# A four-part graph network on one core: dense layers interleaved, stream-back sums copied by ACT and added by GpSimd, third norm in four pieces

## The reference, cut to what matters

```python
# x: (6250, 128); 100000 edges (src, dst), dst sorted; edge_attr (E, 16), type (E,), weight (E,)
x = layernorm(x + segment_sum((x @ W)[src] * (edge_attr @ edge_w), dst) + b)
x = layernorm(x + relu(segment_sum(einsum('ni,rio->nro', x, W1)[src, type] * weight, dst) + bias))
ew = sigmoid(gelu(concat(x[src], x[dst]) @ mlp_w1 + mlp_b1) @ mlp_w2 + mlp_b2)   # self loops get 1
dinv = rsqrt(segment_sum(ew, dst))
x = layernorm(x + segment_sum((x @ conv_w)[src] * dinv[src] * ew * dinv[dst], dst) + conv_b)
h = x
for l in range(4):
    h = relu((h + segment_sum(h[src], dst)) @ W1[l] + b1[l]) @ W2[l] + b2[l]
out = layernorm(x + h)
```

## Time and profile before

| | us |
|---|---|
| median of 3 runs | 4899.19 (4893.37 to 4904.27) |
| the profiled execution | 4892.23 |
| its span | 4890.4 |
| PE busy | 3446.3 (70%) |
| POOL busy | 2407.7 (49%) |
| DVE busy | 2391.9 (49%) |
| ACT busy | 1327.1 (27%) |

### The profile page before, as it was taken

How to read it: one execution, slowest core, us unless ns; L and a number is a source line. 1 busy time by engine, 2 the same in 40 slices (tenths; PEclk the granted TensorE clock), 3 DMA queues, 4 the chain that set the end, 5 groups by cost and what they waited for, 6 DMA issues and landing times. The chain is left out here.

```text
span 4890.4 us, 66925 instructions
## 1 busy us (share of the span) xinstructions
PE 3446.3 (70%) x22480; PEld 2259.6 (46%) x22480; DVE 2391.9 (49%) x5699; ACT 1327.1 (27%) x3055; POOL 2407.7 (49%) x2412
## 2 busy tenths in 40 slices
PE   3888888885666766763333333366769999999997
PEld 3554455553444544542222222266655555555554
DVE  6655555554556556645555555557751030311303
ACT  1232232332222222223444444446650010100101
POOL 3777777765777777757777777721100000000001
PEclk8999999997888888885555555579989999999998
DMA  3343344432333333326777777766767858577674
GB/s 103 106 125 123 122 128 128 135 125 86 93 102 100 100 92 98 102 81 180 201 197 197 199 199 199 201 228 232 245 214 296 307 215 313 217 304 296 226 305 145
DMA packets 509162, 863.95 MB, mean 177 GB/s; under 512 B 111675, under 2 KB 284775, under 8 KB 508868
## 3 DMA queue, kind: packets, MB, share of 16 engines
q1 hardware_dynamic: 345136, 545.24, 31.9%
q0 software_dynamic: 90496, 189.62, 15.2%
q10 hardware_dynamic: 73236, 125.49, 7.0%
HBM read 632.93 MB, written 227.18 MB: 176 GB/s over the span
## 5 line engine op out<-in xcount | busy, mean ns | idle before, releaser
L1604 PE MATMUL psS<-big,xsb 128*128 128x448 f16 x2744 | 971.9, 354 | 16.2 <-issue 8.5
L1604 PE MATMUL psA<-big,xsb 128*128 128x448 f16 x2744 | 971.7, 354 | 0.0
L742 POOL DMA_INDIRECT big<-ht_rows,reli x784 | 787.2, 1004 | 275.0 <-issue 238.6
L742 POOL DMA_INDIRECT big<-xw_rows,srci x784 | 764.0, 975 | 311.2 <-issue 238.6
L769 POOL DMA_INDIRECT big<-axt_rows,srci x784 | 745.7, 951 | 263.2 <-issue 238.5
L1348 PE MATMUL psS<-big 128*128 128x128 f32 x3136 | 501.8, 327 | 317.2 <-DMA big<-ht_rows,reli 315.5
L1348 PEld LDWEIGHTS psS<-big 128*128 128x128 f32 x3136 | 471.8, 238 | 387.9 <-DMA big<-ht_rows,reli 352.5
L1484 PE MATMUL ps<-identh,xsb 128*128 128x128 bf16 x784 | 101.5, 311 | 548.3 <-DVE xsb L2097 548.3
L802 POOL DMA_DIRECT2D x_rows<-y x12 | 11.3, 945 | 962.0 <-DVE y L2355 937.5
L2312 DVE SCALAR_TENSOR_TENSOR acc<-psS,invs,acc 128x448 f32 x56 | 38.3, 684 | 912.0 <-PE psA L1604 912.0
L868 ACT CAST xsb<-ps 128x416 f16<-128x416 f32 x392 | 197.8, 505 | 757.2 <-PE ps L1385 757.2
(11 more groups left out here) (277 smaller groups left out, 5033.0 us busy)
## 6 DMA issues: line engine op xcount, KB each, us to landing
big<-A_rows SPq DMA_DIRECT2D x112, 2744.0 KB, 13.7
A_rows<-xsb ACTq DMA_DIRECT2D x196, 416.0 KB, 2.7
xg_rows<-big SPq DMA_DIRECT2D x98, 512.0 KB, 3.8
big<-xg_rows SPq DMA_DIRECT2D x98, 512.0 KB, 3.7
marks_rows<-big SPq DMA_DIRECT2D x98, 354.0 KB
big<-marks_rows SPq DMA_DIRECT2D x98, 354.0 KB, 4.6
big<-srcq_list SPq DMA_DIRECT2D x98, 256.0 KB
ht_rows<-big ACTq DMA_DIRECT2D x28, 512.0 KB
```

The source lines that it names most:

```text
L742: pool.indirect_dma_start(ring[g % len(ring)][:, j * D:(j + 1) * D], None, table[:, :], bass.IndirectOffsetOnAxis(ap=lists[:, g * TPG + j: ...
L1604: m = pe.matmul(sums, xs[:, t, k, :], Aring[:, r, :, t, :], start=(t == 0), stop=(t == NB - 1))
```

## The change

In the stream-back stage ACT copies the sums of group g-2 out of PSUM after scaling group g (copy_sums), and GpSimd adds them into acc (add_rows); PE's sums of group g wait for that copy. GpSimd's three own-node operations of a chunk now stand at fixed groups among its additions. The third norm's work on DVE is in four pieces at e = 5, 6, 8 and 10 instead of three at 3, 5 and 7, and the transposes back (turn_final, turned_back) are made only where the dense path isn't taken. In their place, an identity product of 32 columns per group in the first two rounds (own_edges) adds each node to its own row of the adjacency matrix.

In the dense layers, all loops over halves are written out, and the hidden and output products of chunk i-1 stand between the large products of half (i, 0) and (i, 1); those of the last chunk stand in the next layer's first half (between). The parts of two layers alternate between two buffers (held). Sums start from the low product by a plain scaling (evict). The scale comes from the previous output's largest value; the transposed output product and GpSimd's stores of x_rows are gone. In the last layer the residual comes back by ACT's DMA and each chunk's final norm follows its output product.

```diff
+        held = [xsb[:, 0:NB * D], acc[:, :]]
+
+        def parts_of(l, c):
+
+            return held[l % 2][:, c * CW:(c + 1) * CW].bitcast(F16).rearrange("p (t k f) -> p t k f", k=2, f=D)
+
+        def summed_in(l, i, r):
+
+            return held[(l + 1) % 2][:, (2 * i + r) * CC:(2 * i + r + 1) * CC]
...
+                def add_rows(g):
+                    b, q = g % 2, g // 2 + R2b.g0
+                    base = pool.value_load(basei[0:1, g:g + 1], min_val=0, max_val=MAXBASE)
+                    pool.wait_ge(r_acc[1 - b], q + (1 if b == 0 else 2))
+                    pool.wait_ge(rows_out, sums_out(g))
+                    at = acc[:, window(base, 0)]
+                    pool.tensor_tensor(at, at, edge_sums[b], ALU.add).then_inc(r_acc[b], 1)
+                for g in range(NG):
+                    add_rows(g)
+                    for c in range(NCH):
+                        if g == own_group(c) + 2:
+                            own_scaled(c)
+                        elif g == own_group(c) + 5:
+                            own_residual(c)
+                        elif g == own_group(c) + 8:
+                            own_biased(c)
...
             def early_n3(g):
 
                 c, e = early(g)
-                if e == 1:
+                if e == 2:
                     act.wait_ge(r_acc[0], R2b.g0 + last_group(c) // 2 + 2)
                     stage_acc(N3, c)
-                elif e == 4:
+                elif e == 7:
                     squares(N3, c)
-                elif e == 6:
+                elif e == 9:
                     root(N3, c)
-                elif e == 8:
+                elif e == 11:
                     store_rows(c)
-                elif e == 9:
-                    turned_back(c)
...
+                def copy_sums(g):
+                    b, q = g % 2, g // 2 + R2b.g0
+                    act.wait_ge(r_seg[b], q + 2)
+                    act.wait_ge(r_acc[b], q + 1)
+                    act.copy(edge_sums[b], psS[b][:, 0:P]).then_inc(rows_out, 1)
                 for g in range(NG):
                     scale_rows(g)
+                    if g >= 2:
+                        copy_sums(g - 2)
                     early_n3(g)
+                for g in range(NG - 2, NG):
+                    copy_sums(g)
...
+            with act.If(dense > 0):
+                act.wait_ge(N3["stored"], NCH + 1)
+                for l in range(LAST):
+                    load_weights(l)
+                    for c in range(NCH):
+                        dense_relu(l, c)
+                        high_part(l, c)
+                load_weights(LAST)
+                fetch_residual(LASTC, 0)
+                for c in range(NCH):
+                    dense_relu(LAST, c)
+                    if c < LASTC:
+                        fetch_residual(c, c + 1)
+                    squares(NF, c)
+                    root(NF, c)
...
+            def own_edges(to, m, k):
+
+                block, part_ = divmod(m, P // TB)
+                if block % KS == k:
+                    at = block // KS * TB
+                    pe.matmul(to[:, at:at + TB], identh[:, :], identh[:, part_ * TB:(part_ + 1) * TB], start=False, stop=False)
...
+                    pe.wait_ge(r_oh[b], it + R2b.g0 + 1)
+                    if g >= 2:
+                        pe.wait_ge(rows_out, sums_out(g - 2))
+                    row_sums(both(back[g % NS]), b, marked)
                     c, e = early(g)
-                    if e == 2:
+                    if e == 3:
                         turn_own(c)
-                    elif e == 8:
-                        turn_final(c)
...
+            def dense_hidden(l, c):
+                lc = l * NCH + c
+                for r in range(2):
+                    pe.wait_ge(a_add[r], (l * NCI + c) * 2 + 3)
+                if c == 0:
+                    pe.wait_ge(l_w, l * 80 + 80)
+                    if l < LAST:
+                        pe.wait_ge(l_scale, scale_step(l, SCALE))
+                if lc:
+                    pe.wait_ge(l_relu, lc)
+                for lo, hi in ((0, 512), (512, CW)):
+                    m = pe.matmul(ps4[:, lo:hi], WA[:, :], hidden_of(l, c)[:, lo:hi], start=True, stop=True)
+                m.then_inc(l_h, 1)
...
+            def between(l, i, r, t):
+
+                if i == 0 and r == 0 and l > 0:
+                    if t == HIDDEN_AT[0]:
+                        dense_hidden(l - 1, NCH - 1)
+                    elif t == PRODUCT_AT[0]:
+                        dense_product(l - 1, NCH - 1)
+                elif i == 0 and r == 1 and l < LAST:
+                    steps = {16: hidden_bound, 24: output_bound, 36: scale_spread}
+                    if l > 0:
+                        steps = {0: largest_turned, 8: largest_spread, **steps}
+                    if t in steps:
+                        steps[t](l)
+                elif i > 0 and r == 0 and t == HIDDEN_AT[1]:
+                    dense_hidden(l, i - 1)
+                elif i > 0 and r == 1 and t == PRODUCT_AT[1]:
+                    dense_product(l, i - 1)
+            with pe.If(dense > 0):
+                pe.wait_ge(n_xn, N3["xn0"] + NCH)
+                for l in range(LAYERS):
+                    for i in range(NCI):
                         for r in range(2):
                             pe.wait_ge(a_ready[r], (l * NCI + i) * 32 + 32)
                             pe.wait_ge(a_add[r], (l * NCI + i) * 2 + 1)
                             for t in range(NB):
-                                if r == 0 and t % CB == 0:
+                                between(l, i, r, t)
+                                if i == 0 and r == 0 and t % CB == 0:
                                     pe.wait_ge(x_lo, l * NCH + t // CB + 1)
                                 for k, sums in enumerate((psS[r][:, 0:CC], low_sums(r))):
-                                    m = pe.matmul(sums, xs[:, t, k, :], Aring[:, r, :, t, :],
+                                    m = pe.matmul(sums, parts_of(l, t // CB)[:, t % CB, k, :], Aring[:, r, :, t, :],
                                                   start=(t == 0), stop=(t == NB - 1))
                             m.then_inc(a_done[r], 1)
...
+                if e == 5:
+                    third_sums(c)
+                elif e == 6:
+                    third_centre(c)
+                elif e == 8:
                     spread_of(N3, c)
-                elif e == 7:
+                elif e == 10:
                     scaled_rows(N3, c, X[:, c * CW:(c + 1) * CW])
...
             with dve.If(more < 1):
-                def finish_rows(g):
-                    b, q = g % 2, g // 2 + R2b.g0
-                    dve.wait_ge(r_acc[1 - b], q + (1 if b == 0 else 2))
-                    dve.wait_ge(r_seg[b], q + 2)
-                    at = acc[:, window(bases[g], 0)]
-                    dve.tensor_tensor(at, at, psS[b][:, 0:P], ALU.add).then_inc(r_acc[b], 1)
-                bases = {}
                 for g in range(NG):
                     b, it = g % 2, g // 2
-                    bases[g] = load_base(it, b)
+                    base = load_base(it, b)
                     edge_scales(b, it, g, g % NS)
-                    row_marks(b, bases[g], 0, it)
-                    if g:
-                        finish_rows(g - 1)
+                    dve.wait_ge(r_seg[b], it + R2b.g0 + 1)
+                    row_marks(b, base, 0, it)
                     early_n3(g)
-                finish_rows(NG - 1)
...
+            def evict(l, i, r):
+
+                dve.wait_ge(a_done[r], l * NCI + i + 2)
+                at, scales = summed_in(l, i, r), invs[:, l % 2, :]
+                dve.tensor_scalar(at, low_sums(r), scales[:, 1:2], None, ALU.mult).then_inc(a_add[r], 1)
+                dve.wait_ge(a_add[r], (l * NCI + i) * 2 + 2)
+                dve.scalar_tensor_tensor(at, psS[r][:, 0:CC], scales[:, 0:1], at, ALU.mult, ALU.add).then_inc(a_add[r], 1)
...
+            def next_parts(l, c):
+
+                lc = l * NCH + c
+                stage, rest, to = blocks(l3stage[lc % 2][:, :]), blocks(rests[lc % 2][:, :]), parts_of(l + 1, c)
+                dve.wait_ge(l_o, lc + 1)
+                dve.tensor_tensor(stage, blocks(ps4[:, 1024:1024 + CW]), spread(l3b2r[:, :]), ALU.add).then_inc(l_xo, 1)
+                dve.wait_ge(l_xo, lc + 1)
+                dve.tensor_tensor(rest, stage, spread(srow[:, :]), ALU.mult).then_inc(x_s, 1)
+                dve.tensor_reduce(mxa[:, c:c + 1], l3stage[lc % 2][:, :], AXX, ALU.max, apply_absolute_value=True).then_inc(l_max, 1)
+                dve.wait_ge(x_hi, lc + 1)
+                dve.scalar_tensor_tensor(to[:, :, 1, :], to[:, :, 0, :], -LOW, rest, ALU.mult, ALU.add).then_inc(x_lo, 1)
...
+            with dve.If(dense > 0):
+                for l in range(LAST):
+                    evict(l, 0, 0)
+                    magnitudes(l)
+                    scales(l)
+                    evict(l, 0, 1)
+                    for i in range(1, NCI):
```

(18 more changed lines are left out.)

389 lines of the change are left out of this document (220 added, 169 removed).

## The result

The changed kernel takes 4773.51 us (median of 4 runs, 4770.63 to 4778.52) against 4897.39 (4 runs, 4893.37 to 4904.27) of the kernel before on the same chip: ratio 0.9746, 95% interval 0.9733 to 0.9759. Forecast was 4809 with a range of 4782 to 4848. The profiled span fell from 4890.4 to 4768.7, by 121.7 us; forecast -87.

What follows compares the result with a forecast made beforehand. Prediction: POOL's gathers bind the sparse rounds, a loop of latencies stream-back, PE the dense layers. Terms sum to -87: 4892.2 becomes 4805 profiled, 4812 with 7.0 for the median; 4809 kept, range 4782 to 4848.

Steps and rivals of the forecast that it cites:

- The copy in the loop: Stream-back: ACT's copy lengthens the two-group loop from 6.65 to 6.95 us, 98 x 0.15 = +15 us (0 to +26).
- The norm in pieces: Stream-back, third norm on DVE: excess per chunk falls from 11.2 to 7.0 us, six chunks, -25 us (-49 to +11).
- the first rival: Norm almost vanishes: excess 3 us per chunk, PE staying at 2.4 GHz; 4785 us, chance 0.13.
- 53 per 14: Sign of being right: 14 stream-back groups with a norm among them take 53 us.
- GpSimd's addition: Stream-back: 0.48 us per 128-column addition, hidden except the last, +0.6 us; sharing with DVE charged only in norm groups, 1.5 per chunk.
- the second rival: GpSimd holds DVE: 24 us over 98 stream-back groups and 16 of the norm's gain lost; 4849 us, chance 0.14.
- Start of the dense stage: Between stream-back and first large product: the ring's first half needs 18.6 us to load, -2 us (0 to -3).
- Gaps (-127) and tail (-47): Dense layers: three gaps of 42.4 us go, -127; six chunks of 7.8 us leave the tail, -47.
- Products on PE: Dense layers: hidden 1.50, output 1.74 and switches 0.4, 3.65 us per chunk, times 27 = +98.5 (+87 to +115).
- Scale products (+5.5) and start of layers (-6): Dense layers: three chains of five tiny products, +5.5 (3 to 10); reduced-clock layer starts and loop jumps go, -6 (-10 to 0).
- The fourth rival: Dense layers: instruction fetch starves PE because large products are written out; slower than before, up to 4977 us, chance 0.04.
- Identity products in the first rounds: First two rounds: one 32-column product per group, hidden under POOL's gathers, 0 us, up to +3.

Runs made afterwards that it cites:

- experiment 2: Changed kernel with ACT copying the sums of group g-2 ahead of the scalings of group g, no longer behind them: ratio 0.9728 to the kernel before.
- experiment 1: Kernel before with DVE loading the next group's base register ahead of its addition of the sums, no longer behind it: ratio 0.9965.
- experiment 4: Changed kernel with DVE again adding the stream-back sums from PSUM, without ACT's copy and GpSimd's addition: 4790.7 us, 279.8 for the 70 norm groups.
- experiment 3: Changed kernel with each hidden and output product cut in two, 108 more switches: 1127.6 us from first to last large product against 1127.5.
- experiment 7: Changed kernel with hidden products at the start of the next chunk's large products and output products four steps later: 4836.7 us.
- 9: Kernel before with PE's spread of group g+2 run before the sums of group g, DVE still adding: ratio 0.9991.
- experiment 10: Changed kernel with PE's spread of group g+2 run before the sums of group g, copy left behind the scalings: 4714.3 us, ratio 0.9619.

## Why the prediction was wrong, step by step

- **The copy in the loop (+15)**: wrong in its sum; quiet groups came at +0. That lies on the bound of 0 that was given, but not for the reason given there. The copy's own part was right in kind (experiment 2, 0.11 a group). What failed is the sentence that the DVE addition "lay in DVE's wait for PE (0.37 before L2194), so taking it away buys nothing in quiet groups". Addition and register load filled that interval themselves; without the load the loop is 0.09 shorter per group (experiment 1), and with the addition gone too the 0.11 of the copy is paid back. Of the error of 35 us this is 15, nearly half, and it is the step whose mechanism was wrong.
- **The norm in pieces (-25)**: measured -31 (289.2 to 265.3 in 70 groups, 42.4 to 35.0 in the last nine). The norm's excess per chunk is 53.05 - 46.6 = 6.4, where 7.0 was charged, and the first rival's 3 is false. The sign "53 per 14" came out, but by luck: it is the walk's 4.0 on a quiet 48.7, while the sum itself, with 7.0, has 55.7; quiet groups 0.15 shorter than forecast and an excess of 6.4 give the same 53. The reason was also another than given: more than half of the gain is DVE's relief from addition and load (14.6 of 23.9 in experiment 4).
- **GpSimd's addition**: the row of the quiet stretch has it at 1.50 us: it stood beside DVE's marks and ended 0.28 behind them, and the marks kept 1.21. Undisturbed it takes 0.41. Where it starts clearly ahead of the marks it is the other way round; the marks, 1.22 otherwise, take 1.33:

```profile
3343.49 0.41 POOL L834 TENSOR_TENSOR acc<-acc,xTs 128x128 f32 x1 [3.05 <-ACT xTs L1182]
3343.65 1.33 DVE L2370 TENSOR_TENSOR xsb<-big,dstf 128x1024 f32<-128x1024 f32 x1
```

Over all 98 groups, as minimum, median and maximum in ns with first and last start, the marks and the addition in the changed kernel, then the marks in the kernel before:

```profile
L2370 DVE TENSOR_TENSOR xsb<-big,dstf x98: 1212/1216/3029, 3235.2 to 3597.4; 128x1024 f32<-128x1024 f32 x98
...
L834 POOL TENSOR_TENSOR acc<-acc,xTs x98: 403/456/1545, 3246.8 to 3602.9; 128x128 f32 x98
```

```profile
L2201 DVE TENSOR_TENSOR xsb<-big,dstf x98: 1212/1216/3045, 3232.0 to 3625.7; 128x1024 f32<-128x1024 f32 x98
```

The marks' median is as before, and what they take beyond it adds up to 10.9 us over all 98, against 10.8 before, nearly all of it beside own-node operations. Additions that start ahead of the marks hold them by some 0.1 us in eight groups; 43 of the 98 additions are themselves stretched beyond 0.5 us, but only one instruction of another engine waited for an addition, ACT's copy of the last chunk, for 0.8 us. So each engine can hold the other, and the second rival's 24 us is false. The Trainium skill ("SBUF — State Buffer", Who interferes with whom) has the lock between the two engines and says that the order of issue decides who waits; in these rows the trace agrees where the starts are clearly apart; the pair at 3266.78 and 3266.79 is too close to tell.

- **Start of the dense stage (-2)**: measured -1.9, 18.6 us from the end of the stream-back work to the first large product, PE waiting for the ring load. But the 2.13 us for the second half of the ring take it back; the forecast had said that PE never waits for the ring.
- **Gaps (-127) and tail (-47)**: right. The tail is 18.9 us, 19 as said.
- **Products on PE (+98.5)**: too much by 16 us. Twenty-seven pairs at 3.06 are 82.6. Of the 0.59 per pair, 0.4 were switches, which cost nothing (experiment 3), and 0.18 came from taking the output product at the 1.74 that the chain prints; between large products it needs 1.56 from its start to the next start.
- **Scale products (+5.5) and start of layers (-6)**: from start to next start the tiny products take 2.3 us in all, below the bound of 3. What is left of 1127.9 after 82.6, 2.3 and the wait of 2.1 is 1041 us, 4 less than four times 261.2, for the second of these.
- **No wait ahead of the inserted products**: right, and shown to hang on the places (experiment 7). The fourth rival, instruction fetch, is false: PE is busy 845.35 of 845.40 us.
- **Identity products in the first rounds (0 to +3)**: the first multiply came 3.2 us later than before, but experiment 1, which has none of them, had it at 3234.59, 3.6 later. So 3 us is what the start differs by without them, and no cost of theirs is shown.

The lower end of the range, 4782, would have held any one of these errors. Three of one sign (15 for the copy, 6 for the norm, 16 for the products) passed it together; the later start of the stage took 3 back. Two of them lay within their own bounds; the third, 82.6, lay below its bound of +87, which took 1.74 for granted.

## What to carry to other kernels

Idle time ahead of an instruction names only what ended last; a register load or an addition on the same engine may fill the same interval. So before an operation is called free, add up both paths into the waiting instruction: where they are nearly equal, shortening the longer one buys only the difference and shortening the other buys nothing (experiments 1 and 9); together they can buy much (experiment 10: 58 us after the exchange). And where a stage is a loop of hand-offs, ask which of its operations needs nothing of the current turn: issuing that one a turn earlier was worth more here (58 us) than all that the change had done in that stage (31.5).
